# Eight layers of attention, experts and a recurrence: the low part of the projections and some routing steps placed elsewhere on VectorE, and the experts' second products in two banks in turn

## What is computed

```
x = x + diff_attention(layernorm(x))                # A1: 8 heads, causal
x = x + gelu_experts(layernorm(x))                  # F1: shared expert + 2 of 8 experts
x = x + causal_attention(layernorm(x))              # A2: 16 heads of 8
x = x + gelu_experts(layernorm(x))                  # F2
x = x + single_head_attention(layernorm(x))         # A3
x = x + block(layernorm(x))    # A4: rmsnorm, full attention (16 heads of 8); F3: swiglu experts
x = x + recurrence(layernorm(x))                    # RR
x = x + block(layernorm(x))    # A5 and F4, with the weights of A4 and F3
```

```
topw, topi = top_k(softmax(h @ router_w), 2)
out = shared(h) + sum over k of w[k] * expert[topi[k]](h)
```

## Time and profile before

| quantity | value |
|---|---|
| median of three runs | 2502.04 us (2498.92 to 2502.05) |
| the profiled execution's own time | 2510.59 us |
| its span, first to last instruction | 2508.9 us |
| mean granted TensorE clock | 0.952 |
| busy: PE / DVE / ACT / POOL | 87% / 69% / 62% / 47% |

### The profile page before, as it was taken

The page is one execution under the profiler, slowest core; times in us unless marked ns, Lnnn a source line. Parts: engine busy times, 40 slices in busy tenths (PEclk is TensorE's granted clock), DMA queues, the critical chain, the costliest instruction groups (busy, mean ns, idle before and its releaser), DMA issues. The chain is left out here.

```text
span 2508.9 us, 59216 instructions
## 1 busy us (share of the span) xinstructions
PE 2188.8 (87%) x18724; PEld 1596.5 (64%) x18724; DVE 1731.3 (69%) x5485; ACT 1561.8 (62%) x3480; POOL 1188.6 (47%) x1685
## 2 busy tenths in 40 slices
PE   7999997999888888998978888899687798887896
PEld 5666665898555555997755555587344455555685
DVE  7788885543688875444867776565887578775565
ACT  5776673576566664675668887333584288885333
POOL 4466664454335555453134664465302245654463
PEclk9999997999899998999989999899898899998998
DMA  8100002123000003223000000222300000002224
GB/s 279 70 8 14 13 14 88 49 71 102 19 2 13 16 16 105 56 71 97 0 6 2 17 16 16 89 75 64 83 1 0 5 2 8 17 17 71 59 73 132
DMA packets 134008, 116.55 MB, mean 46 GB/s; under 512 B 22920, under 2 KB 120214, under 8 KB 131665
## 3 DMA queue, kind: packets, MB, share of 16 engines
q1 hardware_dynamic: 116432, 78.17, 11.0%
q0 software_dynamic: 17280, 34.65, 4.2%
HBM read 58.22 MB, written 56.36 MB: 46 GB/s over the span
## 5 line engine op out<-in xcount | busy, mean ns | idle before, releaser
L1301 ACT ACTIVATE A_Pm<-A_t 128x768 f32<-128x768 f32 (+1 forms) x512 | 468.6, 915 | 152.1 <-PE A_t L1807 148.5
L374 POOL DMA_INDIRECT ybuf<-F_yo,F_idx x284 | 313.2, 1103 | 283.8 <-issue 145.3
L1520 DVE TENSOR_REDUCE A_padm<-A_s 128x4 f32<-128x1024 f32 x256 | 313.0, 1223 | 63.0 <-PE A_s L1799 61.3
L1838 PE MATMUL A_ot<-A_Pm,A_V 128*32 128x256 f32 (+3 forms) x3640 | 299.8, 393 | 15.6 <-POOL A_Pm L1178 14.3
L1807 PE MATMUL A_t<-A_Q,A_K 32*128 32x256 f32 (+1 forms) x2560 | 305.7, 332 | 3.9 <-ACT A_Pm L1301 3.9
L751 PE MATMUL F_hb<-F_xT,F_wt 128*128 128x128 f32 x2272 | 306.9, 278 | 1.9 <-issue 0.8
L227 POOL DMA_INDIRECT xbuf<-xs,dst x256 | 265.2, 1036 | 88.1 <-issue 57.9
L1178 POOL TENSOR_SCALAR_AFFINE_SELECT A_Pm<-A_Pm 128x512 f32<-128x512 f32 x256 | 172.5, 676 | 259.2 <-ACT A_Pm L1301 257.0
L751 PEld LDWEIGHTS F_hb<-F_xT,F_wt 128*128 128x128 f32 x2272 | 275.6, 191 | 12.6 <-issue 7.9
L763 PE MATMUL F_out<-F_WA,F_g 128*128 x1704 | 246.9, 281 | 27.5 <-DVE F_g L578 24.4
L1799 PE MATMUL A_s<-A_K,A_Q 32*128 32x256 f32 (+1 forms) x1536 | 196.5, 332 | 61.2 <-DVE A_padm L1520 47.9
(11 more groups left out here) (461 smaller groups left out, 4877.6 us busy)
## 6 DMA issues: line engine op xcount, KB each, us to landing
F_xr<-xbuf SPq DMA_DIRECT2D x284, 68.0 KB
xbuf<-A_zero SPq DMA_DIRECT2D x16, 1088.0 KB, 17.6
xs<-ybuf SPq DMA_DIRECT2D x32, 512.0 KB, 7.0
ybuf<-F_yo,F_idx POOLq DMA_INDIRECT x284
xbuf<-xs,dst POOLq DMA_INDIRECT x256
F_WA<-in_L_ffn_ew SPq DMA_DIRECT2D x2, 2048.0 KB
F_WA<-in_L_ffn_ew SPq DMA_DIRECT2D x16, 256.0 KB
F_WA<-in_L_ffn_e_gate SPq DMA_DIRECT2D x2, 1024.0 KB
```

The lines of the kernel that those rows point to most:

```text
L374: pool.indirect_dma_start(out=YBUF[:, :], out_offset=bass.IndirectOffsetOnAxis(ap=idx[n][:, h:h + 1], axis=0), in_=yo[r][:, h, :], in_offs ...
L1301: act.activation(Pm[r][:, j:j + 2, :], tbank[:, :].rearrange("p (j k) -> p j k", j=2)[:, :, 0:PW], ACT.Exp, scale=SCALE).then_inc(t_free, 1)
L1520: last = dve.reduce_max(tops.rearrange("p t j -> p j t"), sbank[:, :].rearrange("p (j t k) -> p j t k", j=2, t=TPS), AX)
L1838: last = pe.matmul(obank[h * VG:(h + 1) * VG, 0:NS * SEQ].rearrange("p (s q) -> p s q", s=NS)[:, :, q0:], V[q][:, s, g * QUAD // NS + h, : ...
```

## The change

Three things are changed.

1. `dense_low` leaves the end of the block, where it stood behind `add_y`, and goes into group 0 of the next block, between `with_max` and the second `top`, in A2, A4 and A5. ACT's `squares_of_next` waits for `add_y` of the block before, where it waited for all reads of that block.
2. The table `RSLOT` of A2, A4 and A5 spreads the router's steps over more slots.
3. In the expert stages tile `k` writes its second product into `posb` for even `k` and into `outb` for odd `k`, and waits for the copy of tile `k-2`. The two late blocks of the shared expert both wait for the last tile's copy.

```diff
@@ sparse_expert_stage
+    tile_out = [posb, outb]
@@ VectorE, result(k)
-                o = outb[:, 0:HT * D].rearrange("p (h d) -> p h d", d=D)
+                o = tile_out[k % 2][:, 0:HT * D].rearrange("p (h d) -> p h d", d=D)
@@ TensorE, shared_second(n)
-                if n == NBLK - 1:
+                if n >= EARLY:
                     pe.wait_ge(y_ready, NTILE)
-                elif n >= EARLY:
-                    pe.wait_ge(sh_added, EARLY)
@@ TensorE, tile_second(k)
-                if k >= 1:
-                    pe.wait_ge(y_ready, k)
+                if k >= 2:
+                    pe.wait_ge(y_ready, k - 1)
                 else:
-                    pe.wait_ge(sh_added, EARLY)
+                    pe.wait_ge(sh_added, EARLY - 1 + k)
...
-                        last = pe.matmul(outb[:, h * D:(h + 1) * D], ...
+                        last = pe.matmul(tile_out[k % 2][:, h * D:(h + 1) * D], ...
@@ attention_stage, the table for A2, A4, A5 (a part)
-                 (1, 1, 0): ("counted", "taken"), (1, 2, 0): ("places", "place")}
+                 (1, 1, 0): ("counted",), (1, 1, 1): ("taken",), (1, 2, 0): ("places", "place")}
@@ ScalarE, pair
-                            squares_of_next(b, offset(i, p))
+                            squares_of_next(b, uses[b - 1]["y"] + 1 if b else offset(i, p))
@@ VectorE, pair
                             with_max(n + 1, (g + 1) % NQ, p if g < NQ - 1 else 1 - p, read)
+                        if split and g == 0 and 0 < b < NSEQ - 1:
+                            dense_low(uses[b - 1]["D"], b + 1, shared[uses[b - 1]["D"] % 2])
...
                     add_y(b, use(i, p, "y"), bank_of(i, p, "y"))
-                    if split and b + 2 < NSEQ:
-                        dense_low(use(i, p, "D"), b + 2, bank_of(i, p, "D"))
```

More of the change, by code:

```diff
@@ L756, in tile_second @@
                 pe.wait_ge(g_ready, k + 1)
-                if k >= 1:
-                    pe.wait_ge(y_ready, k)
+                if k >= 2:
+                    pe.wait_ge(y_ready, k - 1)
                 else:
-                    pe.wait_ge(sh_added, EARLY)
+                    pe.wait_ge(sh_added, EARLY - 1 + k)
                 for h in range(HT):
                     for c in range(CH):
-                        last = pe.matmul(outb[:, h * D:(h + 1) * D], g[q][:, c, h * P:(h + 1) * P], w2[:, bass.ds(e, 1), c, :].rearrange("p a d -> p (a d)"), start=c == 0, stop=c == CH - 1)
+                        last = pe.matmul(tile_out[k % 2][:, h * D:(h + 1) * D], g[q][:, c, h * P:(h + 1) * P], w2[:, bass.ds(e, 1), c, :].rearrange("p a d -> p (a d)"), start=c == 0, stop=c == CH - 1)
                 last.then_inc(o_psum, 1)
@@ L1034, in attention_stage @@
     else:
-        RSLOT = {(0, 0, 0): ("first_max",), (0, 0, 1): ("first_gaps", "first_ranks"), (0, 2, 0): ("first_lowest", "first_choice"),
-                 (0, 3, 0): ("others", "second_max"), (1, 0, 0): ("second_gaps",), (1, 0, 1): ("second_ranks", "second_lowest", "second_choice", "chosen"),
-                 (1, 1, 0): ("counted", "taken"), (1, 2, 0): ("places", "place")}
+        RSLOT = {(0, 0, 0): ("first_max",), (0, 0, 1): ("first_gaps",), (0, 1, 0): ("first_ranks",), (0, 1, 1): ("first_lowest",), (0, 2, 0): ("first_choice",),
+                 (0, 3, 0): ("others", "second_max"), (0, 3, 1): ("second_gaps",), (1, 0, 0): ("second_ranks",), (1, 0, 1): ("second_lowest", "second_choice", "chosen"),
+                 (1, 1, 0): ("counted",), (1, 1, 1): ("taken",), (1, 2, 0): ("places", "place")}
         PLACE, NORM = (1, 1), {} if full else {(0, 3, 0): 0, (1, 2, 0): 1}
```

## The result

| comparison (each on one chip) | before, median us | changed, median us | ratio, 95% interval | difference |
|---|---|---|---|---|
| first | 2498.92 (5 runs) | 2483.92 (5) | 0.9927 [0.9909, 0.9946] | 18.2 us faster |
| second (e9_after) | 2499.88 (29) | 2488.78 (12) | 0.9962 [0.9949, 0.9976] | 9.5 us faster |
| third (f1_after) | 2513.81 (11) | 2498.84 (6) | 0.9952 [0.9935, 0.9969] | 12.0 us faster |

The account below looks back on a forecast made before the run. In the attention stages waits in a ring of scores, `top` and exponentials bound it, in gelu tiles PE. Gains of 9.6 us (A4, A5), -0.4 (A2) and 0 (expert tiles) make 9.2 off 2502.04: 2492.8 us, range 2484 to 2502.

Parts of the forecast that it names:

- The ring of `top` and scores: A4: no engine is full; scores, `top` and exponentials wait for each other, costing PE 35 of 260 us.
- the wait of 0.74: Even to odd boundary, full stage: PE waits 0.74 us for a late `top`; moving `dense_low` gains 0.65, 6 times.
- the 0.58 behind it: Even to odd boundary: PE's later wait for ACT's `A_rxT`; the gain is only 0.2 if this merely grows.
- a boundary with logits: Odd to even block from b = 4, full stage: PE is not waiting; moving `dense_low` costs 0.4 us, 6 times.
- the removed wait in the expert tiles: Expert tiles: dropping the wait for the previous copy gains 0, from -1 to +2 us, since `g_ready` implies it.
- The second rival: `dense_low` loses 0.6 at 18 logits boundaries, the other 24 give only 0.2 each: 7.2 us slower, 2509; chance 0.16.
- The first rival: ACT takes the gains: routing steps give nothing, logits boundaries cost 0.6: 1.4 us gained, 2500.6; chance 0.22.
- The third: More is won: routing steps worth 0.21 and 0.67, logits boundaries cost 0.2: about 2485 us; chance 0.12.
- `first_lowest`: Routing step leaving slot (0, 2, 0): gains 0.1 us, 6 times per full stage; costs 0.2, 6 times, in A2.
- One sign of being wrong: Expert layers: the prediction is wrong if one changes by more than 2 us.
- the size of `taken`: Routing step leaving the front of a `top`: 0.35 us of 0.67, 6 times, as ACT idled only 0.25.
- The rule on the shared port: Two-input DVE instructions are locked out beside GpSimd reading SBUF: Mrun's add stays slow, `taken` worth 0.1 instead of 0.35.

Follow-up runs that it names:

- e9_after: The whole changed kernel against the kernel before, a second comparison: 0.9962, 9.5 us faster.
- f1_after: The whole changed kernel against the kernel before, a third comparison on another chip: 0.9952, 12.0 us faster.
- e4: Kernel before with only the two expert-tile banks, still waiting for the copy of the tile just before: 0.9990.
- e11: Kernel before with only the two expert-tile banks and their relaxed waits, run a second time: 0.9996, 1.0 us faster.
- e2: Kernel before with only the routing table `RSLOT` changed: 0.9950, 12.5 us faster.
- e8: Kernel before with only `taken` moved, from slot (1, 1, 0) to (1, 1, 1): one execution, 2507.07 us beside 2515.1, not compared.
- e10: Both attention changes with one bank in the expert tiles, against the kernel before: 0.9955, 11.3 us faster.
- e1: Kernel before with only `dense_low` moved at all 14 boundaries of a stage, with the wait of `squares_of_next`: 0.9961, 9.8 us faster.
- e7: Kernel before with the second product's expert number a constant on PE, not loaded: one execution, swiglu tiles 127.3 and 127.2 us.

## Why the prediction was right and wrong

**Right.** The ring of `top` and scores bounds the stage; the wait of 0.74 was there to be had and the 0.58 behind it did not swallow it; a boundary with logits has nothing to win and loses to the new place; the removed wait in the expert tiles was never the last (e4, e11). A2 comes out near zero, shown +0.8 against -0.4. The second rival (slower) asked for the 24 other boundaries to give less than 0.5 each: those of a full stage's odd blocks give 0.78, and all 24 give 0.62 on average. The first rival (ACT takes the gains) gave the routing steps nothing, and they give 0.80. The third (more is won, 2485) came nearest, with 0.67 for `taken`; but its 0.2 for a boundary with logits and its 0.21 for `first_lowest` were wrong (shown 0.5 and 0). One sign of being wrong, an expert layer that changes by more than 2 us, came up in the first pair of profiles (126.3 to 121.5), and misled: the change did not cause it.

**The step that failed** is the size of `taken`: 0.35 with the reason "ACT would be next". Shown is 0.80 (e2, e8), 12 x 0.45 = 5.4 us more. The argument read ACT's 0.25 us of idle time ahead of one exponential as a limit for the ring. In the changed kernel that exponential starts at 1399.27, 0.93 us behind the scores' start, where it was 0.58 behind the earlier trace rows; it is late by 0.35, and PE's next scores wait 0.22 for it (the row at 1400.43), which takes the offset from -10.76 to -10.48; but the kernel before had 0.28 of idle time just behind that place (at 1411.69), and there the offset is back at -10.83 and stays near it until the next boundary. An idle time is a limit only if what hangs on that instruction is on the ring. And since the old place cost 0.67 and the gain is 0.78, the whole cost was on the path; the 0.11 beyond it is not explained.

The boundary terms were near: +0.78 for +0.65 (0.74 of wait and what stood around it), 1.6 us more over 12; -0.5 for -0.4, 1.2 us less; `first_lowest` 0 for +0.1 in the full stages, 1.2 less, and 0 for -0.2 in A2, 1.2 more.

**The sum** of steps, 15.2 us, lies above the 12.4 of the ratios, and within the 9.5 to 18.2 of the three comparisons. The lengths of whole stages in four profiles of kernels with both attention changes (first, e9, e10, f1) against six with none, over stretches that hold five of the six `taken`, are shorter by 5.7 in A4, 5.0 in A5 and 0.1 to 0.9 in A2 on average, by where its stretch is ended; with the sixth `taken` of each full stage that is 12.4 to 13.2. They scatter by 3 us, and PE's granted clock is part of it. Around 1381 us in e1 (columns as in the earlier trace rows):

```profile
1376.00:1380.00 4.00, 4.00 (x48) 2.72 (x46) 2.09 (x5) 2.83 (x9) 3.80 (x5) 1.00 0.06 19
1380.00:1382.00 2.00, 1.50 (x16) 1.17 (x9) 2.00 (x4) 1.22 (x3) 1.53 (x4) 0.88 0.13 39
1382.00:1384.00 2.00, 2.00 (x20) 1.32 (x23) 1.02 (x5) 1.74 (x4) 0.00 (x0) 0.50 0.00 0
1384.00:1386.00 2.00, 2.00 (x27) 0.79 (x20) 1.12 (x3) 1.07 (x2) 0.00 (x0) 0.77 0.03 8
```

PE had idled 0.5 us, the clock fell to its lower level of 1.2 GHz for some 3 us, and e1's offset rose by 1.2 us there. Such places come and go between executions: e1 has two in A4 (at 1382 and 1532), two in A5 and one in A2 where the first profile of before has none, and these stages end no shorter than before's, though each pair of blocks gains 0.25.

**The first comparison** gave 2483.92, 8.9 us below the forecast of 2492.8. The forecast took its 9.2 from the 2502.04 of three runs; the five runs beside the changed kernel had 2498.92, which makes 3.1 of the 8.9. The missing 6.0 of the steps, 5.4 of them `taken`, make the rest: 2498.92 less 15.2 is 2483.7. The size of `taken` alone would have left the forecast inside its range of 2484.0 to 2502.0 (2492.8 less 5.4 is 2487.4), so that it fell out by 0.08 us is in part the chance of the runs. So is the 18.2 of the ratio: its interval and that of e9, 9.5 with the same two programs, do not meet, and the spread between comparisons is wider than the intervals.

**The rule on the shared port.** By the Trainium skill ("SBUF — State Buffer", "Who interferes with whom") Mrun's add should have stayed slow beside L1207, which reads SBUF too, and by the prediction's estimate `taken` have been worth 0.1. The measurement decides: in the changed kernel it runs from 1398.28 in 0.16 us, inside L1207's 1397.76 to 1398.96. (These are two instructions of 0.60 us, and the add starts 0.09 us before the first ends.) Beside the two-input L1202 it took 0.60 and ended when that ended (1407.85 and 1407.83). Two inputs are not what decides either: in A2 of the kernel before the add took 0.16 us in the middle of a two-input GpSimd instruction on 128x2 elements, which the prediction overlooked when it set A2's 160 ns against the 600:

```profile
828.47 0.72 POOL L1121 TENSOR_TENSOR rs<-A_sq_next,A_half 128x2 f32<-128x2 f32 x1
...
828.70 0.16 DVE L215 TENSOR_TENSOR Mrun<-Mrun,A_Msum 128x8 bf16<-128x8 bf16 x1
```

The delay beside L1202 (128x256) is repeated at all 12 places of A4 and A5, but it does not come with every instruction of GpSimd that reads SBUF, and no run here tells with which.

## What to carry to other kernels

Judge a moved instruction place by place: the same 0.6 us was worth +0.78 where PE waited at the boundary and -0.5 where PE had other work there, and keeping the old place for the second kind gave another 10 us. An engine's short idle time does not cap a gain; follow what hangs on the late instruction. And compare two profiles stage by stage before reading a gain from them: the tiles of F3 and F4, which no edit changed in length, differed by 5 us on average between chips.

## What the runs showed of the hardware

The same program took 2500 us on two chips and 2514 on two others, and the swiglu tiles account for some 5 us of it per layer at a granted clock of 1.00. A bf16 add of 128x8 on DVE took 0.60 us beside a two-input GpSimd instruction on 128x256 elements, and 0.16 beside a one-input one on 128x128 and beside a two-input one on 128x2. PE's signals come about 0.9 us late in 9 to 21 of 71 swiglu tiles, though not because PE loads a number there (e7).
